# A neighbourhood-attention block: three VectorE steps take other places in its hand-written list

## The reference

```
h1  = n1_w * arcsinh(x) + n1_b
q, k, v = split(h1 @ qkv_w + qkv_b)            # 8 heads of 32 channels, q scaled
att = softmax over the 3x3 neighbourhood (clamped at the image's edges) of q.k, times v
h   = x + att @ proj_w + proj_b
h2  = n2_w * arcsinh(h) + n2_b
out = h + gelu(h2 @ mlp_w1 + mlp_b1) @ mlp_w2 + mlp_b2
```

## Time and profile before

| what | value |
|---|---|
| device time, median of 3 runs | 4439.54 us (4438.06 to 4439.81) |
| the profiled execution: its time | 4440.94 us |
| the profiled execution: its span | 4439.1 us |
| busy: PE, DVE, ACT, POOL | 4159.5, 3926.1, 3631.7, 3359.0 us |
| mean granted TensorE clock | 0.992 of full |

### The profile page before, as it was taken

How to read it: one execution, slowest core, us unless ns; L and a number is a source line. 1 busy time by engine, 2 the same in 40 slices (tenths; PEclk the granted TensorE clock), 3 DMA queues, 4 the chain that set the end, 5 groups by cost and what they waited for, 6 DMA issues and landing times.

```text
span 4439.1 us, 129514 instructions
## 1 busy us (share of the span) xinstructions
PE 4159.5 (94%) x49224; PEld 2857.8 (64%) x49224; DVE 3926.1 (88%) x8225; ACT 3631.7 (82%) x5377; POOL 3359.0 (76%) x4092
## 2 busy tenths in 40 slices
PE   5999999999999999999999999999999999999997
PEld 3666666666666666666666666666666666666664
DVE  6899999989989998998999899899989989999984
ACT  4888888888888888888888888888888888888884
POOL 2777777777777777777777777777777777777775
PEclk8999999999999999999999999999999999999998
DMA  4555555555555555555555555555555555555551
GB/s 120 132 141 139 142 139 143 136 139 141 141 140 140 142 137 139 141 140 141 140 142 137 140 141 139 140 141 141 139 139 144 136 140 140 141 141 138 142 133 50
DMA packets 644105, 607.94 MB, mean 137 GB/s; under 512 B 77070, under 2 KB 639376, under 8 KB 639888
## 3 DMA queue, kind: packets, MB, share of 16 engines
q1 hardware_dynamic: 643488, 599.66, 51.2%
HBM read 206.02 MB, written 135.40 MB: 77 GB/s over the span
## 4 chain that ended last, share of the span: by engine, by line
DVE 42%; PE 18%; POOL 13%; issue 13%; ACT 12%; SPq 1%; DMA 0%; POOLq 0%; DVEq 0%; ACTq 0%
PE ps L381 16%; POOL b_lo L1163 6%; POOL b_hi L1161 6%; DVE ps L841 5%; DVE queries L860 5%; DVE o_norm L874 4%; DVE ln_u L767 4%; DVE ln_u L760 4%; DVE k_nat L815 4%; ACT L1073 4%; DVE ln_u L763 3%; DVE h L802 3%; ACT p_hi L1064 3%; DVE q_nat L808 3%; ACT prob L1063 2%
## 5 line engine op out<-in xcount | busy, mean ns | idle before, releaser
L1146 POOL TENSOR_TENSOR p_lo<-prob,p_hi 100x512 f16<-100x512 f32 x1024 | 1269.7, 1245 | 619.1 <-ACT p_hi L1064 619.1
L1063 ACT ACTIVATE prob<-ps 100x512 f32<-100x512 f32 x1024 | 610.2, 596 | 51.1 <-PE ps L381 49.3
L874 DVE TENSOR_TENSOR o_norm<-ps,recip 64x128 f32<-64x128 f32 x2048 | 590.2, 288 | 49.3
L1172 POOL TENSOR_TENSOR g_lo<-g,g_hi 128x512 f16<-128x512 f32 x512 | 593.8, 1160 | 41.0
L1064 ACT ACTIVATE p_hi<-ps 100x512 f16<-100x512 f32 x1024 | 616.4, 602 | 0.0
L381 PEld LDWEIGHTS ps<-v_win,p_hi 100*128 100x128 f16 x8192 | 476.0, 98 | 204.7 <-issue 66.9
L381 PE MATMUL ps<-w_hi,g_hi 128*128 128x256 f16 x2048 | 561.1, 274 | 0.0
L841 DVE TENSOR_REDUCE ps<-ps 128x8 f32<-128x800 f32 x512 | 509.1, 994 | 58.6 <-PE ps L381 54.2
L381 PE MATMUL ps<-w_lo,g_hi 128*128 128x256 f16 x2048 | 560.9, 274 | 0.0
L381 PE MATMUL ps<-w_hi,g_lo 128*128 128x256 f16 x2048 | 560.8, 274 | 0.0
L381 PE MATMUL ps<-v_win,p_hi 100*128 100x65 f16 x8192 | 515.6, 193 | 27.0 <-POOL p_lo L1146 18.4
(11 more groups left out here) (100 smaller groups left out, 11497.9 us busy)
## 6 DMA issues: line engine op xcount, KB each, us to landing
keys<-k_win SPq DMA_DIRECT2D x1536, 100.0 KB, 2.3
v_win<-v_rows SPq DMA_DIRECT2D x1024, 101.6 KB
queries<-q_nat SPq DMA_DIRECT2D x1536, 64.0 KB
v_rows<-v_nat SPq DMA_DIRECT2D x256, 260.0 KB, 4.3
xin<-in_x_dram SPq DMA_DIRECT2D x128, 512.0 KB, 4.3
out_dram<-y SPq DMA_DIRECT2D x256, 256.0 KB, 3.0
queries<-in_query_mask_dram SPq DMA_DIRECT2D x128, 224.0 KB
keys<-in_mlp_w_dram SPq DMA_DIRECT2D x2, 512.0 KB, 6.5
```

The source lines that it names most:

```text
L874: s = v.tensor_tensor(o_norm[r, c], av[r, :, HD * e:HD * e + HD], recip[c % 2][r].to_broadcast([NQ, PAIRS, HD]), ALU.mult)
L1063: act.activation(prob[b][0:NK], ps[0:NK, B_ST + b, :], ACT.Exp, scale=INV * INV).then_inc(prob_ready, 1)
L1146: pool.tensor_tensor(p_lo[b][0:NK], prob[b][0:NK], p_hi[b][0:NK], ALU.subtract).then_inc(p_lo_ready, 1)
L1172: pool.tensor_tensor(g_lo[:, m, :], g32[:, m, :], g_hi[:, m, :], ALU.subtract).then_inc(g_lo_ready, 1)
```

## The change

Only the order of VectorE's list in `step` is changed. Instructions, their operands and their waits stay what they were.

- Slot two: `q_low(t + 2, par, 1)` goes from behind the maxima's copies to ahead of them.
- Slot three: `sum1_(t + 3)` goes from behind the maxima's copies to ahead of them.
- Slot four: `sign1(t + 3, ...)` goes from behind `o_low(t, par, 0)` to ahead of it.

```diff
                     if k == 2 and post:
                         sign2(t - 1, old)
+                    if k == 3 and fill:
+                        sign1(t + 3, (u + 3) % XT)
                     if k == 3 and att:
                         o_low(t, par, 0)
-                    if k == 3 and fill:
-                        sign1(t + 3, (u + 3) % XT)
 
                     if att:
                         sum_reciprocal(t, 2 * k)
                         normalise(t, 2 * k)
+                    if k == 1 and pre:
+                        q_low(t + 2, par, 1)
+                    if k == 2 and fill:
+                        sum1_(t + 3)
                     if more:
                         maxima_to_queries(ta, par if ta == t else old, ka)
 
@@
-                    if k == 1 and pre:
-                        q_low(t + 2, par, 1)
                     if k == 1 and fill:
                         x_from_transposes(t + 3, (u + 3) % XT, 0)
                         x_from_transposes(t + 3, (u + 3) % XT, 1)
@@
-                    if k == 2 and fill:
-                        sum1_(t + 3)
                     if k == 2 and fin:
                         result(t - 2, 0)
```

## The result

The changed kernel takes 4781.2 us (median of 4 runs, 4780.26 to 4781.67) against 4438.8 us (4 runs) before: a ratio of 1.0771, 95% interval 1.0755 to 1.0787, 342 us or 7.7% slower. The forecast was 4766 us. The profiled execution took 4781.67 us, 340.7 more than the one of before.

The account below looks back on a forecast made before the run. VectorE's order of serving the other engines was taken to set the step's length, no engine being full. 124 steps x 2.64 = 327 us on 4440.9 gave 4768, 1.4 lower for the median: 4766 us, range 4620 to 4810.

Parts of the forecast that it names:

- Slot two gives TensorE nothing.: Slot two: Q's low part moves, xT, which the V product awaits, doesn't; TensorE gains 0.00, bounds 0 and 0.91.
- VectorE's own gain of 0.15: Slot two: VectorE's idle 0.15 us ahead of xT's second half goes, but sign2 in slot three swallows it; sum 0.
- The sum is held by b_lo and ends where it did.: Slot three: sum1 comes at 59.48, b_lo runs to 60.55, so sum1 again ends at 61.63; no gain.
- The copies come behind it, and scores_t waits.: Slot three: copies end at 62.53, not 60.25; scores_t on TensorE starts 1.28 us later, TensorE is 0.95 us late.
- The sign is held by p_lo, and o_low behind it holds group 2.: Slot four: p_lo starts 0.25 us before sign1; o_low ends at 68.50, so TensorE's group 2 is 2.77 us late.
- Per step 2.64.: Sum at the gelu of group 3: 2.77 - 0.13 = 2.64 us later in each step, t = 1 to 124.
- The ties: Rival: sign1 gets ahead of p_lo (margin 0.25, 4674 us) or sum1 ahead of b_lo (margin 0.09, 4640); chance 0.14.
- The engines don't block each other: Rival, slots three and four: sum1 and sign1 aren't held; group 2 0.98 late, 0.85 per step, 4545; chance 0.07.
- Faster: Rival, slot two: V's second product starts with x's transposes, up to 0.91 us gained per step, 4327; chance 0.06.
- the rival by the clock: Rival: new waits lower TensorE's clock for groups 2 and 3, 2.6 us more per step, about 5090; chance 0.05.

Follow-up runs that it names:

- the pair: First norm's sum and sign moved as in the change, Q's low part left in its place, against the kernel before: 4766.53 us, ratio 1.0739.
- the exchanged banks: Changed kernel with the banks of the MLP input's groups 2 and 3 exchanged, and the waits that belong to them: 4672.22 us.
- the memset: Changed kernel with GpSimd filling b_lo with zeros by a memset and reading nothing for it: 4685.09 us, ratio 1.0556.

## Why the prediction was right

*Slot two gives TensorE nothing.* Right, and the kernel with that move alone shows it. The sum's term for it, 0, was the one that was mis-sized: it measured 0.12 per step, because the overlap of Q's part and xT was broken up. That is 124 x 0.12 = 15 us, the whole of the gap between 4766 and 4781. The prediction took the order of the copies and Q's part as free ("xT comes after both the copies and Q's part in either order, so it doesn't move"). It was right that VectorE's own gain of 0.15 is swallowed by the second norm's sign, which ends 1.07 after p_lo; the same tie passed on the 0.12.

*The sum is held by b_lo and ends where it did.* Right: 2.09 us, 1.09 after b_lo's end, and 1.23 once b_lo reads nothing. One reading beside it was loose: of b_hi, which lasted 1.61, 0.47 and not some 0.6 came after the sum's end; nothing was worked out from it.

*The copies come behind it, and scores_t waits.* Right: 1.10 us of idle time on TensorE named by the copies, and 96 us for this move alone (94 expected from the same working).

*The sign is held by p_lo, and o_low behind it holds group 2.* Right in both parts. The sign alone and the pair separate them: with the sign 0.22 ahead of p_lo the move costs 120 us, and with the sum's delay it falls 0.27 behind p_lo, which makes up 0.75 of the 0.90 us per step that the pair costs more than the two alone. The kernel with the exchanged banks shows that bank 1 is what ties group 2 to o_low.

*Per step 2.64.* Measured 36.48 - 33.73 = 2.75, with the 0.12 of slot two the forecast's 2.76.

*The rivals.* The ties came out as taken, with 0.16 and 0.27 us. "The engines don't block each other" falls with the sum alone, the sign alone and the memset. "Faster" fell at the row it was said to fall at: TensorE's weights for the V product still waited for xT (1.20 us). The clock stayed at 1.00 with waits of 1.10 and 1.72 us in each step, so the rival by the clock did not come.

## What to carry to other kernels

Before moving an instruction forward, look at what runs on the engine that it shares a path with: an instruction that would be held anyway gains nothing from an earlier place, and what stood in its waiting time is pushed out. Follow each gain to the matmul that should use it and ask which other reader of that PSUM bank it waits for too; in slot two the gain came only once Q's part and xT both went forward. And two moves on one engine aren't additive where a tie of a few tenths of a microsecond, or less, is decided between two engines: in the kernel with the memset it went the other way in every eighth step by 0.07 us and cost 0.76 each time.

## What was unexpected of the hardware

Which neighbours an instruction has changes its price. xT, the reciprocal or o_low start about 0.08 us before the recorded end of a low part or a sign; the maxima's copies start 0.02 to 0.04 us after the end of whatever is ahead of them, and what follows the copies starts 0.02 to 0.04 after theirs. So a swap of two independent instructions cost 0.12 us per step. Why the copies differ was not tried; in the kernel's text they write to partitions from 96 on, Q's part and xT to partitions from 0 on. A GpSimd tensor_tensor of 1.16 us lasted 2.01 when VectorE's instruction came 0.22 us ahead of it, and a tensor_scalar of 0.69 (the magnitude) lasted 0.95 when it came up 0.76 us after a p_lo had started, so the blocking goes both ways and takes in both forms.
